# Attention and a mixture of experts on one core: GpSimd's weight job in two parts, the down product in full blocks, second weights split a stage ahead, the scatter behind the row transposes

## The reference

```python
x = x + layernorm(attn(layernorm(x)))      # 16 heads of 16, rotary turn of q and k, softmax, Wo
x = x + layernorm(moe(layernorm(x)))       # 8 experts of 684 hidden columns, top 2

def moe(x):                                # xs: 4096 tokens x 256
    dist = sqrt(maximum(|xs|^2 + |centroid|^2 - 2 xs @ centroid.T, 1e-12))
    w, sel = top_k(dist, 2); w = softmax(w)
    for e in range(8):
        h = silu(xs @ Wg[e] + bg[e]) * (xs @ W1[e] + b1[e])
        out += we[:, e] * (h @ W2[e] + b2[e])
```

## Time and profile before

| | us |
|---|---|
| median of 3 runs | 1670.2 (1669.54 to 1672.49) |
| the profiled execution, its own time | 1676.76 |
| its span, first to last instruction | 1674.0 |
| TensorE matmuls busy | 1444.0 (86%) |
| VectorE busy | 1112.5 (66%) |
| ScalarE busy | 968.4 (58%) |
| GpSimd busy | 548.2 (33%) |
| mean granted TensorE clock | 0.919 |

### The profile page before, as it was taken

One profiled execution on the slowest core, in us unless ns is written; L12 is line 12 of the kernel. 1 busy time (PEld: TensorE's weight loads), 2 busy tenths in 40 slices (PEclk: granted clock), 3 DMA queues, 4 the chain that ended last, 5 costly groups with the idle time before them and its releaser, 6 DMA issues.

```text
span 1674.0 us, 31840 instructions
## 1 busy us (share of the span) xinstructions
PE 1444.0 (86%) x10413; PEld 893.7 (53%) x10414; DVE 1112.5 (66%) x1890; ACT 968.4 (58%) x1755; POOL 548.2 (33%) x464
## 2 busy tenths in 40 slices
PE   7899969696969889696999862799999999999980
PEld 5454424232323333242334431788888988988970
DVE  7999968696969878696832659355545555555544
ACT  4525867585858767585887542354445444544544
POOL 5740041203040211303131323344444444444424
PEclk9999988797989989897999985899999999999985
DMA  6975444365754635374123952544444444444556
GB/s 201 280 191 91 109 109 137 66 185 131 186 76 152 93 101 88 60 161 75 65 68 83 230 199 125 167 128 118 115 115 125 126 118 119 131 118 116 154 149 204
DMA packets 181487, 220.38 MB, mean 132 GB/s; under 512 B 57583, under 2 KB 152748, under 8 KB 178837
## 3 DMA queue, kind: packets, MB, share of 16 engines
q1 hardware_dynamic: 165493, 200.52, 45.1%
q0 software_dynamic: 15904, 18.66, 6.4%
HBM read 146.64 MB, written 72.48 MB: 131 GB/s over the span
## 4 chain that ended last, share of the span: by engine, by line
PE 50%; DVE 25%; issue 13%; POOL 7%; DMA 2%; SPq 2%; ACT 1%; DVEq 0%; POOLq 0%; ACTq 0%
DVE mx L1084 17%; PE psum L1862 13%; PE psum L1844 5%; PE psum L1842 5%; PE psum L1843 5%; PE psum L1697 4%; PE psum L1670 4%; PE psum L1852 3%; POOL split_raw L884 3%; PE psum L1684 2%; DVE psum L1077 2%; PE psum L1630 2%; PE psum L1644 1%; POOL w_lo L890 1%; PE psum L1771 1%
## 5 line engine op out<-in xcount | busy, mean ns | idle before, releaser
L1466 ACT ACTIVATE work<-psum 128x512 f32<-128x512 f32 x1024 | 544.3, 600 | 200.8 <-PE psum L1684 177.4
L1084 DVE TENSOR_REDUCE mx<-psum 128x1 f32<-128x1024 f32 (+1 forms) x512 | 547.3, 1096 | 47.3 <-PE psum L1670 35.1
L1670 PE MATMUL psum<-stack 48*128 48x512 f32 x1024 | 388.2, 462 | 105.9 <-DVE mx L1084 96.4
L1684 PE MATMUL psum<-stack 50*128 50x512 f32 x1024 | 386.9, 464 | 0.0
L1670 PEld LDWEIGHTS psum<-stack 48*128 48x128 f32 x1024 | 167.4, 193 | 355.0 <-DVE mx L1084 251.9
L1697 PE MATMUL psum<-work,values 128*32 128x384 f32 x4080 | 316.4, 407 | 0.2
L1842 PE MATMUL psum<-w_hi,x_hi 128*128 x568 | 188.4, 332 | 1.0 <-DVE x_lo L1302 1.0
L1844 PE MATMUL psum<-w_hi,x_lo 128*128 x568 | 182.4, 321 | 0.0
L1317 DVE TENSOR_TENSOR h_lo<-psum,h_hi 128x768 fp32r<-128x768 f32 x71 | 68.0, 958 | 171.1 <-ACT h_hi L1551 171.1
L1843 PE MATMUL psum<-w_lo,x_hi 128*128 x568 | 181.6, 320 | 0.0
L1684 PEld LDWEIGHTS psum<-stack 50*128 50x128 f32 x1024 | 166.9, 193 | 24.3 <-ACT work L1466 18.8
(11 more groups left out here) (201 smaller groups left out, 2088.7 us busy)
## 6 DMA issues: line engine op xcount, KB each, us to landing
stack<-qk_scr SPq DMA_DIRECT2D x192, 128.0 KB, 6.2
work<-in_w SPq DMA_DIRECT2D x36, 640.0 KB
small<-in_w SPq DMA_DIRECT2D x35, 640.0 KB
qk_scr<-weights SPq DMA_DIRECT2D x16, 1024.0 KB, 4.7
split_raw<-in_w SPq DMA_DIRECT2D x8, 1368.0 KB
wh_d<-w_hi SPq DMA_DIRECT2D x6, 1368.0 KB, 5.7
w_hi<-wh_d SPq DMA_DIRECT2D x6, 1368.0 KB, 12.0
ot_scr<-weights SPq DMA_DIRECT2D x16, 512.0 KB, 3.2
```

The costliest lines, as they stand in the source:

```text
L1084: dve.tensor_reduce(mx[:, r, a, t:t + 1], scored, AX, ALU.max, negate=True).then_inc(s_max, 1)
L1466: act.activation(pt[u % 4][:, j, :], bank((c + HG * u + n) % 3), ACT.Exp, scale=SC).then_inc(s_exp, 1)
L1670: ins = pe.matmul(bank(4 + 2 * a + half), qs[t3][at:at + QROWS, r, P * t:P * (t + 1)], ks[t3][at:at + QROWS, r, 512 * half:512 * (half + 1 ...
L1684: pe.matmul(bank((t3 + HG * u + n) % 3), ks[t3][at:at + MROWS, r, P * st:P * (st + 1)], qs[t3][at:at + MROWS, r, 512 * half:512 * (half + ...
```

## The change

1. `split_weights(n)` becomes `high_weights(n)` (subtract and high part), called behind `split_max` of r = 1 and ahead of `copy_values`, and `low_weights(n)`, called in the next group behind `split_max` of r = 0.
2. `down` uses 128 rows for the sixth block too; the rows past the 45th hold zeros in `w2`, so they add nothing. Its second product now signals by itself (`s_dh`).
3. `high_w2(t)` moves from tile t + 1 to the end of tile t, waits for `s_dh` of `down(t - 1)` and stands ahead of `save_y` and `high_hidden`. `low_w2` moves to the head of VectorE's tile, ahead of the first `multiply`; `low_hidden` goes behind it.
4. `scatter(t - 2)` now opens GpSimd's tile t, and waits for the row transposes of tile t + 1 (`s_mt`). `y_row` exists twice. `aim_scatter(t - 2)` stands behind `low_hidden(t - 1)`.

```diff
-            def split_weights(n):
+            def high_weights(n):
...
                 for k in range(KC):
                     pool.wait_ge(s_split, split_steps(n, 1) if n == E - 1 else split_steps(n, 0) + k + 1)
                     pool.tensor_copy(high[:, k, :], raw[:, k, :]).then_inc(s_split, 1)
+
+            def low_weights(n):
+
+                at, raw, high = split_in[n], split_raw[split_in[n]], w_hi[:, high_in[n], :, :]
                 for k in range(KC):
...
             def during(i, c):
                 g = over(i, c, 1)
-                if not (isinstance(g, int) and g + 1 >= NG):
-                    for r in range(PAIRS):
+                for r in range(PAIRS):
+                    if not (isinstance(g, int) and g + 1 >= NG):
                         split_max(g + 1, r)
+                    for n, at in enumerate(SPLIT_AT):
+                        if r == 0 and g == at + 2:
+                            low_weights(n)
+                        if r == 1 and g == at + 1:
+                            high_weights(n)
                 if not (isinstance(g, int) and g + 2 >= NG):
                     copy_values(i, c + 2)
-                for n, at in enumerate(SPLIT_AT):
-                    if g == at + 1:
-                        split_weights(n)
...
-            def scatter(t):
+            def scatter(t, p):
+                if not isinstance(t, int) or t + 4 <= NS:
+                    pool.wait_ge(s_mt, t + 4)
                 pool.wait_ge(s_is, t + 1)
                 pool.wait_ge(s_yr, t + 1)
...
+            def tile(t, p):
+
+                if not isinstance(t, int) or t >= 2:
+                    scatter(t - 2, p)
+                if not isinstance(t, int) or t + 3 < NS:
+                    gather(t + 3, 1 - p)
+                if not isinstance(t, int) or t + 2 < NS:
+                    gather_weight(t + 2)
...
             def low_w2(t, p):
                 dve.wait_ge(s_w2h, t + 1)
+                after(dve, s_yp, t)
...
             def high_w2(t, p):
...
-                after(act, s_yp, t)
+                after(act, s_dh, t)
...
-            def save_y(t):
+            def save_y(t, p):
                 act.wait_ge(s_yp, t + 1)
-                after(act, s_ys, 16 * t)
+                after(act, s_ys, 16 * (t - 1))
...
                     for k in range(KH):
-                        rows = P if k < KH - 1 else LAST + 1
-                        last = pe.matmul(bank(7)[:, 0:C], h[0:rows, k, :], w[0:rows, k, :],
-                                         start=n + k == 0, stop=(n, k) == (2, KH - 1))
-                last.then_inc(s_yp, 1)
+                        last = pe.matmul(bank(7)[:, 0:C], h[:, k, :], w[:, k, :], start=n + k == 0, stop=(n, k) == (2, KH - 1))
+                    if n > 0:
+                        last.then_inc((s_dh, s_yp)[n - 1], 1)
```

More of the change, by code:

```diff
@@ L333, in build @@
         x_row = [c.take([C]) for _ in range(2)]
-        y_row = c.take([C])
+        y_row = [c.take([C]) for _ in range(2)]
         mixed = dots_sb[:, 20:22, :].rearrange("p n c -> p (n c)")[:, 0:44].rearrange("p (a b c) -> p a b c", a=2, b=2)
@@ L420, in build @@
         s_hl = sem("hidden_t_low_ready")
+        s_dh = sem("expert_out_of_high_weights")
         s_yp = sem("expert_out_ready")
@@ L875, in norm_o @@
                     pool.tensor_tensor(dims, dims, inverses, ALU.mult).then_inc(s_div, 1)
-            def split_weights(n):
-                p, at, raw, high = n % 2, split_in[n], split_raw[split_in[n]], w_hi[:, high_in[n], :, :]
+            def high_weights(n):
+                p, raw, high = n % 2, split_raw[split_in[n]], w_hi[:, high_in[n], :, :]
                 pool.wait_ge(s_raw[p], 48 * (n // 2 + 1))
@@ L955, in scatter @@
                 pool.indirect_dma_start(out=y_d, out_offset=bass.IndirectOffsetOnAxis(ap=at_y[:, 0:1], axis=0),
-                                        in_=y_row, in_offset=None, compute_op=ALU.add).then_inc(s_ys, 16)
+                                        in_=y_row[p], in_offset=None, compute_op=ALU.add).then_inc(s_ys, 16)
             def gather_weight(t):
@@ L974, in _ @@
             pool.wait_ge(s_wd, 32)
-            for t in range(2):
-                gather(t, t)
-                gather_weight(t)
-            gather(2, 0)
-            gather(3, 1)
-            gather_weight(2)
-            for t in range(1, 2):
-                gather(t + 3, (t + 3) % 2)
-                gather_weight(t + 2)
-                scatter(t - 1)
+            def tile(t, p):
[5 more added lines that the diff above has]
+                    gather_weight(t + 2)
+            gather(0, 0)
+            gather(1, 1)
+            gather_weight(0)
+            gather(2, 0)
+            gather_weight(1)
+            for t in range(2):
+                tile(t, t)
             with pool.Fori(1, (NS - 3) // 2) as i:
                 for p in range(2):
-                    t = 2 * i + p
-                    gather(t + 3, 1 - p)
-                    gather_weight(t + 2)
-                    scatter(t - 1)
-            for t in range(NS - 3, NS + 1):
-                if t + 2 < NS:
-                    gather_weight(t + 2)
-                scatter(t - 1)
+                    tile(2 * i + p, p)
+            for t in range(NS - 3, NS + 2):
+                tile(t, t % 2)
             pool.wait_ge(s_x2r, 16 * (NT // 4))
@@ L1338, in tile @@
                 if not first:
-                    low_hidden(t - 1)
+                    low_w2(t - 1, 1 - p)
                 multiply(t, 0)
                 if not first:
-                    low_w2(t - 1, 1 - p)
+                    low_hidden(t - 1)
+                if not isinstance(t, int) or t >= 2:
+                    aim_scatter(t - 2)
                 multiply(t, 1)
@@ L1350, in tile @@
                     aim_weight(t + 2)
-                if not first:
-                    aim_scatter(t - 1)
             dve.memset(bank(5)[:, P:2 * P], 1.0).then_inc(s_rpad, 1)
@@ L1363, in _ @@
             aim_weight(1)
-            for t in range(2):
-                tile(t, t)
-            with dve.Fori(1, (NS - 3) // 2) as i:
+            for t in range(4):
+                tile(t, t % 2)
+            with dve.Fori(2, (NS - 3) // 2) as i:
                 for p in range(2):
@@ L1370, in _ @@
                 tile(t, t % 2)
+            low_w2(NS - 1, (NS - 1) % 2)
             low_hidden(NS - 1)
-            low_w2(NS - 1, (NS - 1) % 2)
+            aim_scatter(NS - 2)
             aim_scatter(NS - 1)
@@ L1570, in tile @@
                 gate(t, 0)
-                if not first:
-                    high_w2(t - 1, 1 - p)
                 gate(t, 1)
@@ L1575, in tile @@
                     high_x(t + 1)
+                high_w2(t, p)
                 if not first:
-                    save_y(t - 1)
+                    save_y(t - 1, 1 - p)
             high_x(0)
-            for t in range(2):
-                tile(t, t)
-            with act.Fori(1, (NS - 1) // 2) as i:
+            for t in range(4):
+                tile(t, t % 2)
+            with act.Fori(2, (NS - 1) // 2) as i:
                 for p in range(2):
@@ L1586, in _ @@
             high_hidden(NS - 1)
-            high_w2(NS - 1, (NS - 1) % 2)
-            save_y(NS - 1)
+            save_y(NS - 1, (NS - 1) % 2)
             def deviation_mix(u, p):
```

2 lines of the change are left out of this document (1 added, 1 removed).

## The result

The changed kernel takes 1600.4 us (median of 4 runs, 1595.8 to 1608.6) against 1669.9 of before; the ratio is 0.959, interval 0.954 to 0.964. It is faster by 4.1%, some 70 us, where 193 were forecast, and it lies above the range. Its profiled execution took 1608.6 us, its span 1605.8.

What follows compares the result with a forecast made beforehand. Bounds: VectorE's maxima in attention, with stalls for GpSimd's weight jobs; TensorE in the experts' stage. 1676.8 - 106 - 85 - 3 - 2 = 1480.8, less 6.5 is 1474, forecast 1477 us with small losses; range 1460 to 1495 (0.58).

Steps and rivals of the forecast that it cites:

- The weight job: Attention stage: GpSimd's weight job in two parts, run in its idle time, gains 106 us; 7 us stay in one group.
- Rival (c): Attention stage: the first part is late in every weight group, 5 us stay in each of six; 1507 us, chance 0.09.
- Full blocks: Experts' down product: a full sixth block saves 0.40 us for each of 3 products in 71 tiles, 85 us.
- Rival (b): Experts' down product: full blocks save nothing, 1562 us; 1535 to 1600, shared with (a) and (c) together, has 0.12.
- Second weights a stage ahead: Experts' stage: same work on ScalarE and VectorE, earlier second weights; 3 us of stray waits and 2 us of tail saved.
- a ring that the change closes: Experts' stage: second product, high part, low part, multiply, low_hidden, second product; 5.4 us, some 5.6 with hand-overs, against 6.7.
- (a): Experts' stage: the down-product ring binds, its signals held until the scatter ends; 7.1 us a tile, 1505 us, chance 0.17.
- (d): Experts' stage: signals kept back until all three GpSimd DMA instructions are through; ring 9.7 us, 1691 us, chance 0.02.
- late gate-and-up signals: Experts' stage: TensorE's signals seem kept back while the scatter is issued; VectorE's multiply started just behind its end, at 1314.32.
- Stray waits: Experts' stage: 6 us over 70 tiles where a late high part sometimes held TensorE; half, 3 us, taken as saved.
- the tail: End of the experts' stage: TensorE's 2.36 us wait for the high weights goes, 2 us saved.
- The sum: Whole kernel: 1676.8 - 106 - 85 - 3 - 2 = 1480.8; less 6.5 is 1474, forecast 1477 with small losses.

Runs made afterwards that it cites:

- e1: The kernel before with the weight job in two parts alone: ratio 0.937, 1564 us.
- e10: e4 with the bias row issued ahead of the expert's stores and norm_o moved behind the first maximum of groups 10 and 14: ratio 0.884, 1477 us.
- e4: The changed kernel with two slots for the gathered weight and its row numbers, keep_weight a tile later: ratio 0.892, 1490 us.
- e5: e4 with the 45-row sixth block put back: ratio 0.937, 1564 us.
- e7: The changed kernel with SP's load of second weights waiting for keep_weight(t), later in the tile: ratio 0.893, 1491 us.
- e2: The kernel before with the full sixth block alone: ratio 0.979, 1635 us.
- e9: e4 with high_w2 and low_w2 back at their old places: ratio 0.896, 1496 us.
- e12: The changed kernel with high_w2 and low_w2 back at their old places, one weight slot: ratio 0.897, 1498 us.
- e8: e4 with the scatter back behind both gathers, without its wait for the row transposes: 1678 and 1692 us (before: 1677.5 on that chip).
- e6: The changed kernel with VectorE setting the gather's row numbers ahead of keep_weight: ratio 0.901, 1505 us.

## Why the prediction was right in two parts and wrong in one

**The weight job: right.** 106 us forecast, 107.8 in the trace and 106 by e1. Three waits at the transpose as forecast (two near 2.2, and one where the bias row is behind stores; that one took 2.0 us and not 4.5, since the bias row was there 12.4 us behind the maximum, 255.6 to 268.0, and not 14). Rival (c) is out with that: the other weight groups have no wait. `norm_o` kept its cost until e10 moved it.

**Full blocks: right, 12 to 18% too high.** 85 us forecast, 72 to 76 measured by e4 against e5. Rival (b), that they bring nothing, is out: e4 and e5 differ in the rows of the sixth block and in nothing else, and where the gaps go the time goes, if TensorE is the bound. By the rule of the Trainium skill that a load costs by its columns ("TensorE: Matmul & The Clock Gate", section "LDWEIGHTS (loading the stationary operand)") the two would be alike; the measurement decides against that sum.

**Second weights a stage ahead: wrong, and this is the step that failed.** I wrote "same work on ScalarE and VectorE" and, of the scatter, that "both gathers queue behind it, but they are wanted a tile later or more". For the rows that holds. For the slot weight it does not: `keep_weight` and the aims that wait for it stand in VectorE's list, and part 3 put `low_w2` right behind them, so that the weight's landing came to hold the second weights, the product and `h_lo`. I priced a ring that the change closes (through the down product: 5.6 us, or 7.1 lengthened) and not the one that was there: keep, aims, two gathers, landing, keep. It measured 8.0 to 8.4 in the two turns shown, and the tile 8.35 where I had 6.7. Even with that ring noticed its length would have been mis-sized: with the rows of before and the 2.4 to 3.1 us of e7's undisturbed landings it is 1.07 + 0.99 + 0.31 + 2.4 to 3.1, 4.8 to 5.5 us. The order of part 3 lengthened it by two contentions that it caused itself: 1.0 to 1.4 us on the row gather, and some 2 on the landing.

**Rivals (a) and (d): the right kind, the wrong ring.** Their time (1505, 1691) rested on down signals kept back by a scatter; in e4 50 of 50 were not. The late gate-and-up signals were real in the old order: e2 still has them, and with the scatter moved (e9, e12) they are gone and the old order runs at 6.90. But the reason that I gave, a scatter being issued, is not enough for them: in e8 none was late beside one.

**Stray waits and the tail.** With the ring away (e4) the tile is 6.85 over the stage and 6.78 in the steady stretch, so some 5 us of stray waits stay, where I had taken 3 of 6 off. At the end TensorE no longer waits 2.36 us for the high weights, but 1.37 for `h_hi` and 0.61 for `h_lo` in the changed kernel, so of the 2 us of tail 0.4 came. The sum came to 1474, e4 to 1490, 16 above; the blocks account for 9 to 13 of that, and the rest is within the interval of e4's ratio (1479 to 1501).

## What to carry to other kernels

Before an instruction is moved to the head of an in-order list, read what now stands directly ahead of it and what that waits for: here a copy of 0.15 us, whose wait had cost 1.0 us in 71 tiles, cost 104 once a longer instruction stood behind it. List every ring that passes through single buffers (also those of 512 bytes), add up its length, and check what the new order puts beside each of its transfers; a ring with 1.3 to 2 us of slack (4.8 to 5.5 against 6.8) binds when two of its pieces meet a neighbour. And price an edit on TensorE only together with the answer to who bounds the tile after it: the same padded blocks were worth nothing that could be told, 35 and 72 to 76 us in three orders.

## What the runs showed of the hardware

**An indirect DMA on GpSimd is held while VectorE subtracts two operands from SBUF.** Its instruction takes 0.99 us alone. When it starts beside `low_w2` it ends a fixed time behind it: 1207.52 against 1206.66 and 1215.93 against 1215.08 in the changed kernel, and 0.82 to 0.87 us behind it in all 68 row gathers there that start beside it. In the kernel with two slots the row gather starts 0.20 us ahead of `low_w2` and is not held, and the weight gather behind it is:

```profile
1200.68 0.99 POOL L955 DMA_INDIRECT values<-xn_d,at_x  x1 [0.30 <-issue]
1201.98 1.49 POOL L971 DMA_INDIRECT w_slot<-w_d,at_w  x1 [0.30 <-issue]
...
1200.88 1.76 DVE L1333 TENSOR_TENSOR w_lo<-work,w_hi 128x1536 fp32r<-128x1536 f32 x1 [1.97 <-ACT w_hi L1566]
```

It ends at 1203.47, 0.83 us behind 1202.64. The products and `h_lo`, with one operand in PSUM, hold nothing: in the changed kernel 69 weight gathers run beside one of them or beside `low_x`, and take 0.94 to 0.96 us. The Trainium skill ("SBUF — State Buffer", section "Who interferes with whom") says that a VectorE instruction with two SBUF inputs contends with a GpSimd instruction that reads SBUF; the indirect DMA, which reads its row numbers there, behaves like one in this trace.

**A gather of 512 bytes lands later beside a load of 684 KB.** From the end of its instruction to VectorE's copy it is 3.6 to 4.3 us in the changed kernel, where SP issues the load at the same moment, and 3.8 to 4.4 in the turns of e6 where it does so; 1.5 to 1.8 in the turns of e6 without a load beside it, and 1.5 to 2.1 in the 8 turns of e7 with the load begun 2.2 to 3 us before it.

**Loads of 45 rows among loads of 128** cost 0.34 us a product, as measured by the tile (e4 against e5). The rows of before show the gaps around such a load; what makes them, no run shows.

What stays open is why TensorE's gate-and-up signals come late beside a scatter in the kernel before and in e2, and in time in e8; the down product's came in time wherever a run could show it (e4, e5). No run separated them.
